# Row maxima of the attention by pairs of heads, one on each row half of TensorE, with a new order of the steps and new loads

## What is computed

```python
q, k, v = (x @ Wq.T, x @ Wk.T, x @ Wv.T)        # each as (batch, head, 1024, 8)
attn = softmax((q @ k.T) * 128 ** -0.5)         # over the 1024 keys
attn = attn + rel_bias                          # added after the softmax
out = attn @ v                                  # then a layer norm, gamma, beta
```

## Time and profile before

| what | us |
|---|---|
| runs shown: median (lowest to highest) | 714.29 (712.39 to 714.3) |
| the profiled execution, its own time | 714.63 |
| its span in the trace | 712.8 |
| TensorE busy | 667.4 |
| VectorE busy | 531.1 |
| ScalarE busy | 379.4 |
| attention groups 0 to 7 in the trace | 251 to 640 |

### The profile page before, as it was taken

How to read it: one execution, slowest core, us unless ns; L and a number is a source line. 1 busy time by engine, 2 the same in 40 slices (tenths; PEclk the granted TensorE clock), 3 DMA queues, 4 the chain that set the end, 5 groups by cost and what they waited for, 6 DMA issues and landing times.

```text
span 712.8 us, 9213 instructions
## 1 busy us (share of the span) xinstructions
PE 667.4 (94%) x3314; PEld 277.7 (39%) x3314; DVE 531.1 (75%) x952; ACT 379.4 (53%) x688; POOL 91.3 (13%) x96
## 2 busy tenths in 40 slices
PE   7898999899997899999999999999999998998997
PEld 5453545444573633232232332332322322334443
DVE  6569788836699867878878878888888887309744
ACT  3735233333203057766766757776777678872231
POOL 5920210001044501020020000000000002002000
PEclk9999999999999999999999999999999999999999
DMA  8000000000313102012010010010010000000011
GB/s 242 26 0 0 1 0 1 1 0 0 115 69 128 62 30 97 1 40 87 3 52 16 3 61 7 8 62 2 26 42 2 1 1 2 1 1 0 1 29 29
DMA packets 19309, 22.31 MB, mean 31 GB/s; under 512 B 3264, under 2 KB 11968, under 8 KB 19264
## 3 DMA queue, kind: packets, MB, share of 16 engines
q1 hardware_dynamic: 17872, 20.94, 8.9%
q0 software_dynamic: 144, 0.52, 0.2%
q10 hardware_dynamic: 1248, 0.27, 0.2%
HBM read 17.33 MB, written 4.19 MB: 30 GB/s over the span
## 4 chain that ended last, share of the span: by engine, by line
PE 70%; DVE 20%; ACT 4%; issue 2%; DVEq 1%; DMA 1%; POOL 1%; ACTq 0%; POOLq 0%
PE banks L1456 18%; PE banks L1379 15%; PE banks L1442 14%; DVE negmax L1054 7%; PE banks L1181 6%; PE banks L1259 4%; PE banks L1302 3%; PE banks L1250 2%; DVE arena L912 2%; ACT arena L755 2%; PE banks L1194 2%; DVE arena L962 1%; PE banks L1393 1%; DVE arena L914 1%; PE banks L1498 1%
## 5 line engine op out<-in xcount | busy, mean ns | idle before, releaser
L1054 DVE TENSOR_REDUCE negmax<-banks 128x1 f32<-128x1024 f32 x256 | 301.0, 1218 | 57.1 <-PE banks L1379 56.4
L755 ACT ACTIVATE arena<-banks 128x512 f32<-128x512 f32 x512 | 270.0, 602 | 128.4 <-PE banks L1442 125.2
L1379 PE MATMUL banks<-arena 72*128 72x512 bf16 x512 | 154.1, 382 | 14.3 <-DVE negmax L1054 13.9
L1442 PE MATMUL banks<-arena 75*128 75x512 bf16 x512 | 157.7, 380 | 4.3 <-ACT arena L755 3.6
L1456 PE MATMUL banks<-arena 128*32 128x512 f32 x1024 | 136.4, 605 | 0.7 <-ACT arena L755 0.7
L1379 PEld LDWEIGHTS banks<-arena 72*128 72x128 bf16 x512 | 37.1, 97 | 143.6 <-issue 60.4
L1442 PEld LDWEIGHTS banks<-arena 75*128 75x128 bf16 x512 | 48.3, 97 | 95.8 <-ACT arena L755 53.7
L514 POOL TENSOR_TENSOR rstd<-veps,neghalf 128x4 f32<-128x4 f32 (+1 forms) x24 | 27.1, 1128 | 286.7 <-DVE veps L826 236.1
L1259 PE MATMUL banks<-arena,bT 128*128 128x512 f32 x128 | 60.1, 593 | 1.6 <-ACT arena L608 1.6
L608 ACT ACTIVATE arena<-banks 128x512 f32<-128x512 f32 (+1 forms) x56 | 32.1, 595 | 49.4 <-PE banks L1181 20.6
L912 DVE TENSOR_SCALAR arena<-banks,bi 128x512 f32<-128x512 f32 x32 | 23.9, 745 | 33.0 <-PE banks L1259 33.0
(11 more groups left out here) (137 smaller groups left out, 640.5 us busy)
## 6 DMA issues: line engine op xcount, KB each, us to landing
arena<-qk_scratch SPq DMA_DIRECT2D x192, 48.0 KB
arena<-in_tab SPq DMA_DIRECT2D x4, 1024.0 KB, 6.9
qk_scratch<-arena SPq DMA_DIRECT2D x8, 384.0 KB, 2.6
out<-x SPq DMA_DIRECT2D x4, 256.0 KB, 2.3
x<-in_x POOLq DMA_DIRECT2D x1, 512.0 KB, 8.1
arena<-nm_part SPq DMA_DIRECT2D x24, 8.0 KB, 1.9
x<-in_x ACTq DMA_DIRECT2D x1, 256.0 KB, 3.8
x<-in_x SPq DMA_DIRECT2D x1, 256.0 KB, 3.4
```

What stands on the lines that cost most here:

```text
L755: act.activation(probs[s % 2][:, h, :], score_bank(g, n), ACT.Exp, scale=SCALE).then_inc(exp_done, 1)
L1054: return dve.tensor_reduce(negmax[:, buf, k:k + 1], slot.rearrange("p a b -> p (a b)"), axis=AXX, op=ALU.max, negate=True)
L1379: last = pe.matmul(slot[:, half_, :], qs[0:STACK, buf, h, t * P:(t + 1) * P], ks[0:STACK, buf, h, half_ * HALF:(half_ + 1) * HALF], start= ...
L1442: pe.matmul(score_bank(g, n), ks[0:DEPTH, g % BUFS, h, t * P:(t + 1) * P], qs[0:DEPTH, g % BUFS, h, q * HALF:(q + 1) * HALF], start=True, ...
```

## The change

- **Maxima by pairs.** An item is now one half of the keys for two heads: two products of 128x512 with 64 rows of contraction each, one on rows 0 to 63 of the array and one on rows 64 to 127 (`UPPER = 64`), into the two banks of the slot. The 64 rows leave out the product of the third part of q with the third part of k; the scores keep all 72. VectorE reduces the slot to two numbers a row instead of one, into `negmax_part`, and with a group's last item takes the lesser of the two (negated) halves. A group still has 32 items.
- **Rows for the pairs** are separate tiles (`pair_rows`, in space of x0, oT and the old parts) with loads of their own, four DMAs a head. The products of the scores are now loaded in two DMAs of 72 rows a head instead of six of 24. With that SyncE still issues 24 DMAs a group. For group 0 the pair rows of heads 1 and 3 are issued by ScalarE, behind its last copy of the first experts. `store_parts` has five DMAs instead of four, and its first waits for both halves of q.
- **Order.** `plan` deals out two maxima to each step, one between scores 1 and 2 and one behind the weighing; the four scores stand before the weighing; `bias` stands directly behind a weighing, and `bias_turn`, `turn` and `out` between score 3 and the weighing.
- **Waits.** The first maxima of a pair wait for `pairs_loaded` of both heads, the first scores of a group for `products_loaded`.

```diff
-RING = NEXT_MAXES[:4] + [("bias", 0, 0), NEXT_MAXES[4], ("bias_turn", 0, 0)] + NEXT_MAXES[5:] + AFTER_NEXT + [("out", 0, 0)]
+BIAS_STEP, BIAS_TURN_STEP, TURN_MAXES_STEP, OUT_STEP = 2, 4, 11, 15
...
+    maxes = NEXT_MAXES + [("max", 2, k) for k in range(EARLY)]
+    steps = []
+    for j in range(STEPS):
+        after_scores, after_weighing = [], []
+        if bias and j == BIAS_STEP:
+            after_weighing.append(("bias", 0, 0))
+        if bias and j == BIAS_TURN_STEP:
+            after_scores.append(("bias_turn", 0, 0))
+        if deepest and j == TURN_MAXES_STEP:
+            after_scores.append(("turn", 1, 0))
+        if j == OUT_STEP:
+            after_scores.append(("out", 0, 0))
+        first, second = maxes[2 * j:2 * j + 1], maxes[2 * j + 1:2 * j + 2]
+        steps.append([[x for x in part if x[1] <= deepest] for part in (first, after_scores, after_weighing, second)])
+    return steps
...
+        pair_words = [x0[:].rearrange("p b t c -> p (b t c)"), words_0[:, 0:2 * S], oT[:].rearrange("p b t -> p (b t)")]
+        pair_rows = [m.bitcast(BF16).rearrange("p (w h t) -> p w h t", w=2, h=GH // 2) for m in pair_words]
...
+        def load_pair_rows(engine, G, buf, h):
+            mine, base, pair = rows_of_head(G, h), UPPER * (h % 2), h // 2
+            high, low = slice(base, base + HIGH_ROWS), slice(base + HIGH_ROWS, base + UPPER)
+            q, k = q_rows[mine, :], k_rows[mine, :]
+            engine.dma_start(pair_rows[buf][high, 0, pair, :], q[0:(NPART - 1) * HD, :].unsqueeze(1).broadcast_to([(NPART - 1) * HD, NPART, S])).then_inc(pairs_loaded[buf][h], 16)
+            engine.dma_start(pair_rows[buf][high, 1, pair, :], k.unsqueeze(0).broadcast_to([NPART - 1, NPART * HD, S])).then_inc(pairs_loaded[buf][h], 16)
+            engine.dma_start(pair_rows[buf][low, 0, pair, :], q[(NPART - 1) * HD:, :].unsqueeze(1).broadcast_to([HD, NPART - 1, S])).then_inc(pairs_loaded[buf][h], 16)
+            engine.dma_start(pair_rows[buf][low, 1, pair, :], k.rearrange("(d n) t -> d n t", n=NPART)[:, 0:NPART - 1, :]).then_inc(pairs_loaded[buf][h], 16)
         @block.sync
         def _(sp):
...
-                for k in range(4):
-                    which, h = k // 2, k % 2
-                    sp.wait_ge(qk_low, 4 * b + k + 1)
-                    sp.dma_start(scratch[which, :, b * P:(b + 1) * P, h * HALF:(h + 1) * HALF].rearrange("n p t -> p n t"),
-                                 qk_part[b][:, which, :, h * HALF:(h + 1) * HALF]).then_inc(qk_stored[b], 16)
-                sp.wait_ge(qk_stored[b], 64)
+                mine = slice(b * P * NPART, (b + 1) * P * NPART)
+                sp.wait_ge(qk_low, 4 * b + 2)
+                for i in range(NPART):
+                    sp.dma_start(q_rows[mine, :].rearrange("(h n d) t -> n h d t", n=NPART, d=HD)[i], qk_part[b][:, 0, i, :]).then_inc(qk_stored[b], 16)
+                for h in range(2):
+                    sp.wait_ge(qk_low, 4 * b + 3 + h)
+                    sp.dma_start(k_rows[mine, h * HALF:(h + 1) * HALF].rearrange("(p n) t -> p n t", n=NPART),
+                                 qk_part[b][:, 1, :, h * HALF:(h + 1) * HALF]).then_inc(qk_stored[b], 16)
+                sp.wait_ge(qk_stored[b], 16 * STORES)
             def load_products(G, buf):
                 for h in range(GH):
-                    head = bass.ds(G * GW + h * HD, HD)
-                    for i in range(NPART):
-                        rows = slice(i * NPART * HD, (i + 1) * NPART * HD)
-                        sp.dma_start(qs[rows, buf, h, :], scratch[0, i, head, :].unsqueeze(0).broadcast_to([NPART, HD, S])).then_inc(products_loaded[buf][h], 16)
-                        sp.dma_start(ks[rows, buf, h, :], scratch[1, :, head, :]).then_inc(products_loaded[buf][h], 16)
+                    if G or h % 2 == 0:
+                        load_pair_rows(sp, G, buf, h)
+                for h in range(GH):
+                    rows = rows_of_head(G, h)
+                    sp.dma_start(qs[0:STACK, buf, h, :], q_rows[rows, :].unsqueeze(1).broadcast_to([NPART * HD, NPART, S])).then_inc(products_loaded[buf][h], 16)
+                    sp.dma_start(ks[0:STACK, buf, h, :], k_rows[rows, :].unsqueeze(0).broadcast_to([NPART, NPART * HD, S])).then_inc(products_loaded[buf][h], 16)
...
+            act.wait_ge(qk_stored[0], 16 * STORES)
+            for h in range(1, GH, 2):
+                load_pair_rows(act, 0, 0, h)
...
-                return dve.tensor_reduce(negmax[:, buf, k:k + 1], slot.rearrange("p a b -> p (a b)"), axis=AXX, op=ALU.max, negate=True)
+                pair, t, q = k // (2 * NT), k // 2 % NT, k % 2
+                last = dve.tensor_reduce(negmax_part[:, buf, q, 2 * pair:2 * pair + 2, t], slot, axis=AXX, op=ALU.max, negate=True)
+                if k == MAXES - 1:
+                    dve.drain()
+                    last = dve.tensor_tensor(negmax[:, buf, :], negmax_part[:, buf, 0].rearrange("p h t -> p (h t)"),
+                                             negmax_part[:, buf, 1].rearrange("p h t -> p (h t)"), ALU.min)
+                return last
...
-                h, t = k // NT, k % NT
-                if t == 0:
-                    pe.wait_ge(products_loaded[buf][h], (G + d - buf) * (16 * 2 * NPART // BUFS) + 16 * 2 * NPART)
-                for half_ in range(2):
-                    last = pe.matmul(slot[:, half_, :], qs[0:STACK, buf, h, t * P:(t + 1) * P], ks[0:STACK, buf, h, half_ * HALF:(half_ + 1) * HALF],
+                pair, t, q = k // (2 * NT), k // 2 % NT, k % 2
+                for side in range(2):
+                    h, rows = 2 * pair + side, slice(UPPER * side, UPPER * (side + 1))
+                    if t == 0 and q == 0:
+                        pe.wait_ge(pairs_loaded[buf][h], ((G + d) // BUFS + 1) * 64)
+                    last = pe.matmul(slot[:, side, :], pair_rows[buf][rows, 0, pair, t * P:(t + 1) * P], pair_rows[buf][rows, 1, pair, q * HALF:(q + 1) * HALF],
                                      start=True, stop=True)
                 return last
...
+                if n < GH:
+                    pe.wait_ge(products_loaded[g % BUFS][h], (G // BUFS + 1) * 32)
...
-            def step(G, g, s, fill_item, ring):
-                scores(G, g, s, 0)
-                if len(ring) > 0:
-                    fill_item(ring[0])
-                scores(G, g, s, 1)
-                scores(G, g, s, 2)
+            def step(G, g, s, fill_item, beside):
+                first, after_scores, after_weighing, second = beside
+                for h in range(GH // 2):
+                    scores(G, g, s, h)
+                for k in first:
+                    fill_item(k)
+                for h in range(GH // 2, GH):
+                    scores(G, g, s, h)
+                for k in after_scores:
+                    fill_item(k)
                 if s:
                     weigh(G, g, s - 1)
-                elif not (isinstance(G, int) and G == 0):
+                elif G:
                     weigh(G - 1, g - 1, STEPS - 1)
-                if len(ring) > 1:
-                    fill_item(ring[1])
-                scores(G, g, s, 3)
-                for k in ring[2:]:
+                for k in after_weighing + second:
                     fill_item(k)
```

49 lines of the change are left out of this document (27 added, 22 removed).

## The result

The changed kernel takes **716.61 us** in the median (714.4 to 721.51), the kernel before 714.11 us on the same chip (712.39 to 718.25): ratio 1.0033, interval 1.0018 to 1.0047. It is a little slower. 704.0 us were forecast; the measured time lies inside the range, and the gain that was forecast is not there.

A forecast was written before the change was run, and what follows sets the result against it. It took TensorE to bound the regular step before, and ScalarE's loop, a hair over TensorE, after. Terms -9.6 - 3.2 - 0.4 + 0.9 + 2.0 = -10.3 us gave 704.0 us; range 698 to 712 at 0.50, 691 to 724 leaving out about 0.19.

The forecast's parts named there:

- The start: Before the first maxima: the first item waits for head 1's rows and nothing gives the delay back, +2.0 us (1 to 4).
- the landing: Head 1's loads at the start: last issued at 194.2, landed at 196.8, by a store's 2.5 to 2.6 us.
- The last two groups: Groups 6 and 7 beside regular steps: third item gone -0.6, first copy 0.35, three later copies 0.4 each; +0.9 us.
- The regular step: One attention step, weighing to weighing: 2.74 us by ScalarE's loop, 0.09 less than now; 107 steps give -9.6 us.
- The halves overlap: An item's two 64-row products take one product's time, 0.218 us; rival without overlap: step 3.15, kernel 748 us, chance 0.06.
- the pair of changes at an item: Array division changed into and out of a half-row item on TensorE: 0.084 + 0.12 = 0.204 us a pair.
- a score to be filled: Last term of ScalarE's loop, between the weighing's or item's end and the next exponential: 0.42 us.
- What lies beside the steps: Bias group beyond its 16 steps: bias, out, turns, small waits and take_pv copies, 4.58 against 5.38 us; four groups -3.2.
- The changes were not dearer: Slower rival: array changes at 0.17 us each, step 2.99, kernel 731 us; range 713 to 740, chance 0.22.
- free: Faster rival: changes by rows almost free, ScalarE's loop sets the step at 2.62, kernel 691 us; chance 0.12.
- the split maxima: Rival: 72-row loads issue slowly on SyncE, so split maxima come late for the next group's first score; 740 us, chance 0.05.
- the gain eaten by waits on VectorE and the start: Case in which waits on VectorE and the start use up the gain: 712 to 716 us, chance 0.05.

The follow-up runs named there:

- head1_alone: Changed kernel, but SyncE issues head 0's pair rows, then waits for head 1's to land before other loads; ScalarE issues head 1's alone: 712.33 us, ratio 0.9953.
- weigh_before_score3: Changed kernel with the old order inside a step (weighing ahead of score 3, second item behind it), halves and dealing kept: 706.33 us, ratio 0.9908.
- after: The changed kernel itself, with the whole change, against the kernel before: 716.61 us, ratio 1.0033.
- one_wait_of_exp0: Changed kernel without ScalarE's wait, at the head of each step, for the weighing whose probabilities exponential 0 overwrites: 710.4 us, ratio 0.9957.
- dealing_alone: Kernel before, with whole-array maxima, old loads and old order inside a step, plus only the new dealing of items and extras to steps: 713.31 us, ratio 0.9983.
- before3_early: Changed kernel with the weighing ahead of score 3, second item behind it, and head 1's loads issued ahead of ScalarE's last copy: 701.13 us, ratio 0.9806.
- sync_rows_first: Changed kernel, but SyncE issues all four heads' pair rows of group 0 ahead of the 72-row loads and ScalarE none: 711.44 us, ratio 0.996.
- together_alone: Changed kernel with adjacent items, head 1's loads early, exponential 0's second wait removed, head 2's and 72-row loads held until head 1's land: 698.34 us, ratio 0.978.
- act_rows_early: Changed kernel with head 1's four pair-row loads issued ahead of ScalarE's last work of the sweep before; head 3's stay: 712.95 us, ratio 0.9973.
- dummies_sized: Changed kernel with 40 instead of 14 dummy products on TensorE ahead of the first item: 714.52 us, ratio 0.9994.

## Why the prediction was wrong, point by point

The forecast was -10.3 us, the profiles say +2.3. The 12.6 us between them lie in three places.

- **The start, +2.0 forecast, +7.4 measured: 5.4 of the error.** The step that failed is the landing: it was taken from the stores' 2.6 us, and the rows landed 7 us after their last issue, with the rows of heads 2 and 3 and the 72-row loads in flight beside them. head1_alone has 3.45 us with only head 0's rows before it. The last of the four issues came at 193.79, forecast 194.2, partly by luck: the four began beside the copy and not behind it (191.09), and one of them took 1.24 us instead of 0.73. What was not in the list at all: the wait leaves TensorE without work, its clock falls to half, and the stretch up to the first score, which had been called bound by VectorE and so untouched, grows. It is 3.0 us longer than at full clock (56.80 against 53.84), and 1.2 longer than in the kernel before, which has the second of the two falls itself. The 7.4 are 6.45 us for the later reduction and 1.20 for the stretch, less 0.22 as the copy itself came sooner.
- **The last two groups, -0.1 forecast (+0.9, less 1.0 for eleven steps), +4.3 measured: 4.4 of the error.** The forecast saw the three copies there and gave them 0.4 us each. It did not ask what the new place of the weighing does to every other piece of TensorE work that stands between two steps. With score 3 ahead of the weighing, ScalarE idles through weighing and extra; the earlier trace rows held the loop from which this could have been read. weigh_before_score3 takes 83.0 us for these two groups where after takes 89.3 and before 85.0.
- **Groups 0 to 5, -12.2 forecast (their 96 steps at -0.09, and -3.2 and -0.4), -9.4 measured: the other 2.8.** The regular step, 2.74 forecast and 2.78 measured, makes 3.8 of it, and group 0 gave 1.0 back. TensorE's own part was right: 2.72 forecast, 2.72 in one_wait_of_exp0. The halves overlap, and the pair of changes at an item, 0.204 us forecast, is 0.206; its parts, 0.084 in and 0.12 out, are 0.10 and 0.10, so that the errors cancel. That ScalarE's loop would set the step was right too. The step that failed is its term for "a score to be filled", 0.42 where 0.49 stood: it was read in the earlier trace rows from exponential 3, which has one wait, and the new order puts exponential 0 there, which has a second, for the weighing (one_wait_of_exp0). The Trainium skill, "TensorEngine Tiling (Array Packing)", section "Key Properties", says that a change of the tiling mode drains TensorE; the rows on row halves now agree, with 0.10 us each way. It speaks against five changes a step, and the cost it warns of was in the sum.
- **What lies beside the steps** came out about right in sum, for reasons that were partly wrong. For a bias group 4.58 us beside 16 steps were forecast, and 49.18 - 16 x 2.78 = 4.70 were measured. The parts differ: `out` costs 1.18 (0.88 forecast), `turn` and `bias_turn` 0.41 and 0.52 (0.11 and 0.44, and 0.1 for a wait at each of the three), and of the two copies one shows its 0.36 us as forecast (0.35) while the other lies in the step of `out`. It was said that the crowded steps go with the dealing, and dealing_alone shows that the dealing by itself gives nothing (50.68 us). The saving beside the steps needs the new place of the extras or the halves. Groups 1 to 3 came out at -1.5 us each instead of -2.2, groups 4 and 5 at -1.6 together instead of -3.3, mostly by the step's 0.04. Group 0, with the first steps in it, gave -3.2 instead of -2.2.

Of the rivals none is the one that came. The changes were not dearer, nor free, the halves overlap, and the split maxima were not late. The case that came is nearest to "the gain eaten by waits on VectorE and the start", one of the two given 0.05, and even that named neither the landing, nor the clock, nor the late part. The range held the time because it reached to dear changes, which did not happen.

Of what the change is named for, the halves are worth what was worked out: -0.11 us a step in both orders, some 5 to 7 us of the time with the old order (706.33 against 713.31 by the medians, 0.9908 against 0.9983 by the ratios), although that run pays the slow start in full. What made the whole slower came with it and needs none of it: the weighing moved behind score 3, a wait that this brings onto the path, and loads from two queues on the way to the first item.

## What to carry to other kernels

When an order is rewritten, look at every piece that stands between two rounds of the loop, not at the regular round alone, and ask of each what the other engine has in hand while it runs; here the last score behind the weighing was that stock. A transfer that the first instruction of a phase waits for should be priced with all that is issued around it, on any queue, and its wait with what an idle TensorE does to its clock afterwards. Try the parts of a change one at a time: here the change without its new order inside a step gives 1% (weigh_before_score3), and with the loads issued early 2% (before3_early), where the whole gave nothing. And before a difference is put down to an edit, compare the granted clock of the two executions: 1.6 us of such a difference here were a fall that came in one profile and not in the other.

## What the runs showed of the hardware

- A change between the whole array and row halves costs 0.10 us into the halves and 0.10 us out; two 64-row products of 512 columns on the two halves take the time of one (0.39 us).
- A second wait ahead of an exponential for which ScalarE stands idle costs 0.06 us if it is fulfilled only shortly before the wait that counts (0.49 against 0.43 us from score to exponential). What it costs if it was fulfilled long before is not shown.
- The loads of head 1's rows had landed 3.45 to 3.8 us after the last of them was issued when no other queue was issuing at the time (head1_alone, sync_rows_first), and 5.6 to 7 us when two were (together_alone, act_rows_early, after). A load of 72 rows takes 0.72 to 0.78 us to issue, hardly more than one of 24 rows (0.68), but single issues took longer: 1.15 to 1.43 us ScalarE's first load of 48 rows of k, in head1_alone too, and 1.80 and 2.87 us two of SyncE's in after.
- The granted clock fell to half behind a wait of TensorE of 2.3 us in head1_alone (0.50 from 198 to 202) and of 1.6 us in together_alone (0.66 from 198 to 202), and stayed up behind one of 1.9 us in sync_rows_first and behind 1.9 and 0.3 us in act_rows_early: by these runs the length of the wait alone does not tell. It also falls near 236 to 240, in a stretch that VectorE bounds, with an earlier fall (after) or without one (before, dealing_alone, dummies_sized), and there the longest pause of TensorE just before was 1.1 us (before) and 1.3 us (dummies_sized). sync_rows_first has the same pause of 1.3 us and no fall; what decides it isn't settled.
